# Expert rows fetched by token number, found by one-hot products, and the attention's work moved to other steps

## What is computed

```
xn = layernorm(x)
gnn: h = xn @ W;  out[col] += h[row] * dinv[row] * dinv[col]  over the edges and self loops
mix: q, k, v = xn @ w_qkv + b_qkv;  A = q k^T * SCALE
     numerator = 1 + A + 0.5 A*A;   attn = numerator / numerator.sum(-1)
     out = (attn v) @ w_proj + b_proj
x = x + gnn + mix
xf = layernorm(x)
probs = softmax(xf @ switch_w + switch_b);  prob_max, routes = max, argmax
rank = position of the token among those of its expert, by falling prob_max
keep = rank < 195
buf[route, rank] = xf                  (kept tokens only)
h = gelu(buf @ w1 + b1);  o = h @ w2 + b2
y = o[route, rank] where kept, else xf
x = x + y * prob_max
```

## Time and profile before

| | us |
|---|---|
| median of 3 runs | 1110.61 (1110.03 to 1113.11) |
| the profiled execution | 1114.51 |
| its span | 1112.6 |
| TensorE busy in the span | 933.1 (84%) |
| VectorE busy | 773.2 (69%) |
| ScalarE busy | 483.2 (43%) |
| GpSimd busy | 342.0 (31%) |

### The profile page before, as it was taken

The page is one execution under the profiler, slowest core; times in us unless marked ns, Lnnn a source line. Parts: engine busy times, 40 slices in busy tenths (PEclk is TensorE's granted clock), DMA queues, the critical chain, the costliest instruction groups (busy, mean ns, idle before and its releaser), DMA issues.

```text
span 1112.6 us, 15566 instructions
## 1 busy us (share of the span) xinstructions
PE 933.1 (84%) x5250; PEld 887.4 (80%) x5250; DVE 773.2 (69%) x1557; ACT 483.2 (43%) x710; POOL 342.0 (31%) x223
## 2 busy tenths in 40 slices
PE   3897789989989989989998779699999983197885
PEld 3896778878878978878987679699999982197885
DVE  6778168889878889878887635646676666067673
ACT  2221256656656656656667402112232222154540
POOL 2025555544546546534344000000000002323342
PEclk9898899999999999999999889899999995599898
DMA  8966443283273273285463374554545424786761
GB/s 235 350 181 144 85 88 49 36 153 56 28 153 49 35 153 52 32 173 118 120 133 70 47 164 108 135 134 110 146 114 144 109 70 152 214 268 213 232 223 45
DMA packets 139572, 142.44 MB, mean 128 GB/s; under 512 B 71418, under 2 KB 119133, under 8 KB 138503
## 3 DMA queue, kind: packets, MB, share of 16 engines
q1 hardware_dynamic: 110628, 125.01, 42.7%
q0 software_dynamic: 28496, 16.68, 10.3%
q10 hardware_dynamic: 403, 0.17, 0.1%
HBM read 99.09 MB, written 42.97 MB: 128 GB/s over the span
## 4 chain that ended last, share of the span: by engine, by line
PE 51%; DVE 16%; issue 12%; DMA 9%; ACT 8%; POOL 1%; SPq 1%; DVEq 0%; ACTq 0%; POOLq 0%
PE ps L1872 12%; PE ps L1874 11%; PE ps L1873 11%; PE ps L1166 6%; PE ps L1150 3%; PE ps L1151 3%; ACT Ph L812 3%; DMA out<-oE,ids 3%; DVE Pl L1024 3%; DMA vdram<-VS 3%; ACT Pf L834 2%; DVE Ph L1022 2%; PE ps L1520 1%; DMA Cs<-counts 1%; DVE oE L1806 1%
## 5 line engine op out<-in xcount | busy, mean ns | idle before, releaser
L372 POOL DMA_INDIRECT counts<-countc,idxu x157 | 273.5, 1742 | 299.8 <-DMA counts<-countc,idxu 204.7
L1024 DVE SCALAR_TENSOR_TENSOR Pl<-Pf,Ph 125x832 fp32r<-125x832 f32 (+1 forms) x180 | 184.4, 1026 | 65.0 <-ACT Ph L812 58.9
L834 ACT ACTIVATE Pf<-ps 125x832 f32<-125x832 f32 (+1 forms) x180 | 155.8, 866 | 147.1 <-PE ps L1151 140.1
L1166 PE MATMUL ps<-Ph,vsb 125*128 125x416 f32 (+1 forms) x360 | 132.1, 367 | 10.4 <-DVE Pl L1024 10.1
L1166 PE MATMUL ps<-Pl,vsb 125*128 125x416 f32 (+1 forms) x360 | 127.8, 355 | 0.0
L1663 POOL DMA_INDIRECT rows<-XF,slots x10 | 14.7, 1470 | 337.3 <-DVE slots L1479 334.6
L1872 PE MATMUL ps<-XH,wqkH 128*128 128x416 f32 (+1 forms) x216 | 81.3, 376 | 19.6 <-DVE R L942 9.9
L1872 PE MATMUL ps<-wH,XH 128*125 128x384 f32 x240 | 84.7, 353 | 10.5 <-DVE OHL L969 5.8
L1166 PEld LDWEIGHTS ps<-Ph,vsb 125*128 125x128 f32 x360 | 68.9, 191 | 20.7 <-DVE Pl L1024 10.6
L1873 PE MATMUL ps<-wL,XH 128*125 128x384 f32 x240 | 83.4, 348 | 0.0
L1874 PE MATMUL ps<-wH,XL 128*125 128x384 f32 x240 | 83.2, 346 | 0.0
(11 more groups left out here) (247 smaller groups left out, 2243.5 us busy)
## 6 DMA issues: line engine op xcount, KB each, us to landing
Cs<-counts SPq DMA_DIRECT2D x20, 546.9 KB
w1s<-L_ffn_w SPq DMA_DIRECT2D x8, 1152.0 KB
w2s<-L_ffn_w SPq DMA_DIRECT2D x8, 1152.0 KB, 5.7
odram<-OHL SPq DMA_DIRECT2D x12, 625.0 KB, 8.5
oS<-odram SPq DMA_DIRECT2D x10, 750.0 KB, 4.8
vdram<-VS SPq DMA_DIRECT2D x10, 672.0 KB
vsb<-vdram SPq DMA_DIRECT2D x12, 560.0 KB
kt<-keyd SPq DMA_DIRECT2D x5, 1280.0 KB, 6.0
```

What stands on the lines that cost most here:

```text
L372: pool.indirect_dma_start(out=counts, out_offset=bass.IndirectOffsetOnAxis(ap=idxu[:, c:c + 1], axis=0), in_=countc[:, c:c + 1], in_offset ...
L834: act.activation(Pf[:, i % RING, :, 0:w], ps[0:T, 2 * (i % 2):2 * (i % 2) + 2, 0:w], ACT.Square, bias=1.0).then_inc(sq_done, 1)
L1024: dve.scalar_tensor_tensor(out=p, in0=f, scalar=1.0, in1=h.bitcast(F32), op0=ALU.add, op1=ALU.subtract).then_inc(p_lo, 1)
L1166: ins = pe.matmul(ps[:, 4 + s % 2, 0:w], vsb[:, 2 * kp + t, a, :], part[:, m % RING, t, 0:w], start=(kp == 0 and t == 0 and part is Ph), s ...
```

## The change

1. **Routing.** The seven operations for `slots` and the ten scatters to `rows` go. For each of the ten tiles VectorE writes `seat`, 125 tokens by 195 places, one where the token's rank is that place; TensorE multiplies it with the one-hot experts times token number and times top probability (`lg[:, 1:3]`, 16 columns), accumulated over the ten tiles, once for each of the two row tiles, and a one-row product adds 2097152 to the token numbers, which `tok` carries negatively, so that an empty place has a number out of bounds. VectorE casts the result to `ids` for all eight experts and copies `pmc`.
2. **Rows.** SyncE stores each tile of `XF` to the DRAM array `xfd` during the node tiles (`store_rows`); GpSimd gathers an expert's rows from it by `ids` (`fetch_rows`): experts 0 and 1 at the start, expert e+2 at the start of turn e, where SyncE had loaded them before. `rows`, `blank`, `clear` and the `r_zero` waits go.
3. **Order at the node tiles' end.** `add_ranks` and `compare` of the tiles before come ahead of the last tile's `logits` and `choose`; in `choose` the probability comes before the expert.
4. **Experts.** VectorE no longer waits for `oe_store` before `w2L`, only at `oE`; the copies of ids are replaced by one small operation on `pcur`. `w1L` of expert 0 comes first, and the `pads` wait for `plain_store`.
5. **Attention.** The step tables change, and all three quadratic products use bank 6, so that the first projection step waits for the queries' reading (`kq_full`) instead of the second quadratic's (`r_done`).

The diff, cut to its core:

```
-        XF, = right(ctx, [("XF", [T, NT, RW], F32)])
+        XF, = right(ctx, [("XF", [T, NT, D], F32)])
...
-            sp.wait_ge(consts, 1)
-            sp.dma_start(blank.rearrange("(p d) -> p d", p=2), zeros[0:2, 0:RW]).then_inc(r_zero, 16)
-            sp.wait_ge(r_zero, 16)
-            sp.dma_start(blank.rearrange("(p d) -> p d", p=2)[:, D + 1:RW], iota_f[0:2, 10:11],
-                         allow_slow_non_contiguous=True).then_inc(r_zero, 16)
...
-        QUAD_AT, TOTAL_AT, INVERSE_AT = (3, 5, 8), (11, 12, 13), 16
-        PROJ_AT, TURN_AT, GRAM_AT = (7, 13, 20, 24, 29), (24, 27, 30), 32
+        QUAD_AT, TOTAL_AT, INVERSE_AT = (1, 5, 9), (13, 14, 15), 18
+        PROJ_AT, TURN_AT, GRAM_AT = (7, 13, 19, 25, 30), (24, 27, 30), 32
...
-        READ_AT = (11, 16, 23, 27, 32)
+        READ_AT = (11, 16, 22, 28, 33)
...
-        FIRST_AT = (24, 25, 26, 28)
-        LATE_AT = (2, 5)
+        FIRST_AT = (23, 25, 26, 29)
+        LATE_AT = (0, 5)
...
-                        if i == PROJ_AT[0]:
-                            pe.wait_ge(r_done, 3 * j + 2)
+                            pe.wait_ge(kq_full, 6 * j + 6)
...
+            def store_rows(i):
+                sp.wait_ge(xf_done, i + 1)
+                move(sp, xfd[i * T:(i + 1) * T, :], XF[:, i, :], xf_store)
...
+            add_ranks(NT - 3)
+            compare(NT - 2)
...
             logits(NT - 1)
             choose(NT - 1)
-            add_ranks(NT - 3)
-            compare(NT - 2)
             add_ranks(NT - 2)
             compare(NT - 1)
             add_ranks(NT - 1)
...
+            for i in range(NT):
+                dve.tensor_scalar(seat[:, i, :], place[:], rank[:, i:i + 1], None, ALU.is_equal).then_inc(seat_done, 1)
+            for t, (r0, n) in enumerate(CTILES):
+                dve.wait_ge(seat_mm, t + 1)
+                dve.tensor_copy(ids[0:n, t, :], ps[0:n, 2 * t, 0:E]).then_inc(ids_done, 1)
...
+            for t, (r0, n) in enumerate(CTILES):
+                for i in range(NT):
+                    pe.wait_ge(seat_done, i + 1)
+                    pe.matmul(ps[0:n, 2 * t, 0:2 * E].rearrange("p (a e) -> p a e", a=2), seat[:, i, r0:r0 + n], lg[:, 1:3, i, :],
+                              start=(i == 0), stop=False)
+                pe.matmul(ps[0:n, 2 * t, 0:2 * E], later[0:1, 1:1 + n], far[:].rearrange("p a e -> p (a e)"), start=False,
+                          stop=True).then_inc(seat_mm, 1)
...
-            for i in range(NT):
-                pool.indirect_dma_start(out=rows, out_offset=bass.IndirectOffsetOnAxis(ap=slots[:, i:i + 1], axis=0),
-                                        in_=XF[:, i, :], in_offset=None, bounds_check=SLOTS - 1, oob_is_err=False
-                                        ).then_inc(sent, 16)
...
+            def fetch_rows(e):
+                for t, (r0, n) in enumerate(CTILES):
+                    pool.indirect_dma_start(out=xe[0:n, e % 2, t, :], out_offset=None, in_=xfd,
+                                            in_offset=bass.IndirectOffsetOnAxis(ap=ids[0:n, t, e:e + 1], axis=0),
+                                            bounds_check=N - 1, oob_is_err=False).then_inc(xe_in[e % 2], 16)
...
             for e in range(E):
+                if e + 2 < E:
+                    pool.wait_ge(xe_tr, 3 * e + 3)
+                    fetch_rows(e + 2)
...
-                        dve.wait_ge(oe_store, e + FREE)
-                        ids_of(e + 1, 1 - b, m * 32 + 32 * (b + 1))
+                        dve.wait_ge(oe_done, 2 * e + FREE)
+                        chance_of(e + 1, 1 - b)
                         split_w2(e + 1, 1 - b)
```

146 lines of the change are left out of this document (67 added, 79 removed).

## The result

| | before | after |
|---|---|---|
| median, us | 1111.46 (1110.03 to 1113.11, 4 runs) | 1080.79 (1076.30 to 1081.14, 4 runs) |
| profiled execution, us (span) | 1114.51 (1112.6) | 1076.30 (1074.5) |
| mean granted clock of TensorE | 0.937 | 0.952 |

The ratio is 0.9714, with a 95% interval of 0.9685 to 0.9744: 31 us faster. That is inside the range given for 8 in 10 (1044 to 1083), outside the forecast's own (1051 to 1072), 19 us above the predicted time and 4 above rival A's. The profiled execution of after is 4.4 us faster than the other three, which lie within 0.5 us of each other. The mean granted clock of those three is 0.942 to 0.946, and six experiments have profiles of the same attention code; by these the 4.4 us are most likely the clock of the attention. (The change of clock meant here is between 1.0 and 0.5 of full speed, 2.4 and 1.2 GHz.)

The account below looks back on a forecast made before the run. TensorE was taken to bound node tiles and nearly the attention, a circle through the results' landing the expert turns. Gains of 22 + 1 + 15 + 11 = 49 us gave 1110.6 - 49 = 1061.6 us; own range 1051 to 1072, 8 in 10 1044 to 1083.

Parts of the forecast that it names:

- rival A: Attention: VectorE becomes the bound, only 7 us of wait MA stay, the rest returns as waits for Pl; 1076.6 us, 18%.
- attention, five turns: Attention turns with a projection: 4.1 us gained in each of five, from moving work off three TensorE waits.
- routing: Last router logits to first expert: place products and gathers replace scatters and load; 15 us gained, bounds 10 and 18.
- experts: Expert turns: w2L leaves the circle, turns of 15.3 instead of 17.47 us; 11 us gained, bounds 2 and 18.
- I take 4.1 of the 5.7 us: Attention: share of the 5.7 us a turn expected to stay, since VectorE, at 88% of the turn, is late next.
- The three waits: TensorE in the attention: for MA at step 5 (1.5 us), R at step 7 (2.0), kt at the gram product (1.2).
- The 1.0 us of clock a turn: Attention: granted clock falls to 0.50 behind the wait for R; removing that wait regains 1.0 us a turn.
- the last argument: Experts: the second store, issued later beside a weight load, lands in a little less than 6.4 us; 15.3 taken.
- Rival B: Experts: GpSimd's queue is the bound, w1L holds the first store every turn, nothing gained there; 1072.6 us, 12%.
- Rival C: Whole kernel: everything runs at TensorE's pace, 67 us gained; 1043.6 us, 13%.
- Rival D: Experts: the two new gathers delay each store by two landings of 6.1 us, circle 26.5 us; 1127 us, 1%.
- The signs of being wrong: Edge-count scatters ending behind the attention, node tiles over 192 us, or gathers landing only after 955.

Follow-up runs that it names:

- a_load: The changed kernel with three compares of edge keys done twice, at steps 7, 8 and 10 of a pair: 1099.28 us.
- b_again: The kernel before, unchanged, run once more for a second profiled execution: 1110.33 us.
- r_fill: The changed kernel with GpSimd's two fills of xe behind the ten seat operations instead of beside the last tile's choice: 1080.01 us.
- e_behind: The changed kernel with the two gathers of expert e+2's rows behind the stores and x1 gathers instead of ahead of the first store: 1135.43 us.
- e_ahead: The changed kernel with the two row gathers at the end of GpSimd's turn, for expert e+3 instead of e+2: 1078.59 us.
- e_w1late: The changed kernel with w1L of the next expert behind the three hL in VectorE's turn instead of ahead of them: 1081.39 us.
- r_free: The changed kernel with w1L of the first expert and the last two plain rows ahead of the casts of ids: 1079.13 us.
- e_wait: The changed kernel with w2L again behind the landing of the results of the expert before: 1094.34 us.
- a_later: The changed kernel with compares of edge keys moved from steps 7 to 10 to where VectorE has gaps: 1075.38 us.

## Why the prediction was right in its range and wrong in its size

| step | predicted gain | measured |
|---|---|---|
| first stage | 1 | 1.7, likely (108.6 to 106.9) |
| attention, five turns | 20.5 | 8.5 (422.1 to a median of 413.7) |
| attention, last turn | 1.5 | 1.2 (73.2 to 72.0) |
| node tiles | 0 | 0 within scatter |
| routing | 15 | 11.3 (55.2 to 43.9) |
| experts | 11 | 9.0 (17.47 to 15.67 a turn, five turns) |
| sum | 49 | 31.7; the medians say 31 |

**Attention, the step that failed: "I take 4.1 of the 5.7 us".** The three waits went as described, some 23 us in the five turns (the earlier trace rows without the waits for `MA` of the first pair and of the last turn). What failed is what was late next. The prediction named VectorE with 88% of the turn, and then let the 58.9 us for which VectorE idled for `Ph` speak for room; the 4.1 itself stands on no row. Only some of those microseconds lie in steps 3 to 13, where TensorE was to come forward. The largest of them stands at step 9. Timeline of DVE before, in the second turn and in the third, where the clock had fallen:

```profile
250.88 1.03 DVE L1024 SCALAR_TENSOR_TENSOR Pl<-Pf,Ph 125x832 fp32r<-125x832 f32 x1 [2.72 <-ACT Ph L812]
...
335.34 1.03 DVE L1024 SCALAR_TENSOR_TENSOR Pl<-Pf,Ph 125x832 fp32r<-125x832 f32 x1 [4.28 <-ACT Ph L812]
```

The waits for `MA` and `R` that were removed ahead of it are 3.5 us a turn, more than the gap of 2.7; with the clock, about 5 against 4.3. In after that gap is used up, VectorE has none from step 3 to 13, and a_load shows that a microsecond added there costs TensorE a whole one. So 14 of the 23 us came back as waits for `Pl`, `kt` and `inv` (idling fell from 39.0 only to 30.2): 1.7 us a turn were kept, not 4.1. That is rival A in its mechanism for steps 3 to 13, VectorE the bound with waits for `Pl`, and nearly in its size (7 us for the whole attention against 9.7). Behind step 13 the waits for `inv` and for `kt` ahead of the transposes grew by some 3 us each, which A doesn't explain; their cause stays open.

**The 1.0 us of clock a turn** The earlier trace rows was counted as regained because its wait, for `R`, goes. It was read in one turn and taken for all five. The clock fell in three of them, for some 3 us each, and in two in b_again; with about 1.5 us a fall, 1.0 a turn comes out for the first profile by luck. Windows of 5 us in the third turn, of r_fill and then of after:

```profile
335.00:340.00 5.00, 5.00 (x26) 4.87 (x26) 2.69 (x6) 1.76 (x2) 3.09 (x2) 0.77 0.44 79
```

```profile
335.00:340.00 5.00, 5.00 (x34) 4.95 (x33) 3.64 (x8) 2.64 (x3) 3.15 (x2) 1.00 0.42 79
```

In r_fill the clock falls behind the new wait of 1.3 us at step 13, in three turns of five; in e_behind, e_ahead, e_w1late and r_free also in three, in e_wait in two, in the profiled execution of after in none. TensorE's busy time in the five turns is 383.5 in r_fill, 384.1 before: this gain wasn't had. It is as large as the 4.4 us by which the profiled execution of after beats the other three, and a_later, whose wait at step 13 is at most 0.67, has it.

**Routing: 15 predicted, 11.3 measured, from errors of both signs.** The place products took less than 9.3 us: 6.97 for 40 of the 44 records, and `ids` were complete 8.4 us behind the ranks instead of 10.1, 1.7 better. The ranks came only 0.5 us earlier, not 1.9, and r_fill shows why: the fills of `xe`, costed at nothing without naming who runs beside them, held one small VectorE operation for 2.6. From `ids` to the transposes it is 13.6 us instead of 9.5, 4.1 worse: the hold of the first gather was foreseen, but the second one started 5.8 us behind `ids`, and its landing took 7.7 us instead of the median of 6.1; r_free, without the hold, has 10.7. Part of the 4.1 is a slip in the sum: it has the gathers issued by 948.4, so the second at 947.4, and the median landing makes that 953.5, not the 951.8 that it goes on with. By its own rows it was 13.3 us, not 15. Together 1.7 - 1.4 - 4.1 = -3.8. The bounds, 10 to 18, held; the sign given for `ids`, 7 us behind the ranks, wasn't the sum's 10.1, and 8.4 lies between.

**Experts: mechanism right, 9.0 us of the 11.** `w2L` left the circle (e_wait puts it back and pays 2.7 us a turn), the first store slipped into `w1L` in every turn but the first, TensorE's waits for `oE` are 1.2 to 1.8 us (under 2, as said), and 15.7 us lie between the 15.3 chosen and the 15.8 that the sum gave before the last argument, that the second store would land sooner. That argument wasn't borne out, and for the 0.15 in the sum the prediction gives no row. Rival B had the first store right, but not that this takes all. Rival C needed free stores: e_ahead has the first one free and comes to 14.3 us a turn. Rival D said that a gather delays a store behind it by its landing; in after the stores land 6.5 us (median) from their issue, with two gathers in front, so it doesn't. But e_behind shows the other side of the same choice: put last, the gathers are on TensorE's path, and the turn is 24.4 us.

The Trainium skill, "SBUF — State Buffer", section "Who interferes with whom", infers that writing descriptors needs the write interface of the pair that VectorE and GpSimd share; by that inference `w1L` would have held none of these transfers. The rows contradict it once more (4.23 us beside `w1L` in after, 1.00 in e_w1late where `w1L` runs elsewhere), and the sum was right to go by the row.

**The median and one profile.** The prediction subtracted from the median, which was right. The two profiled executions alone would say 38 us; 4.4 of these are most likely the clock of the attention in one of them, and 3.1 are that the other was that much slower than its median.

**The signs of being wrong.** None came: the last scatter of edge counts is issued at 585.7 us, 29 before the attention's end (600.49 and 31 before); the stretch with the node tiles takes no longer than before; the first gathers have landed by 937. The turns of the attention were to take 79 to 80 us and take 82.7.

## What to carry to other kernels

When waits of one engine are removed, look at the engine that is next by place, not by sum: draw its timeline over the very steps from which work is moved, and count the gaps there. Idle time elsewhere in the turn isn't room, and a gap at the very place is room only up to its own length. Where a transfer is placed in a queue, price it both ways: what it delays behind it, and when its own reader wants it. With the same two gathers the turn is 15.7 us where they stand ahead of the stores, 24.4 where they stand behind them, and 15.0 (14.2 to 14.5 from the third turn on) where they stand behind but are fetched a turn earlier. And small fills on an engine that idles aren't free if they hold an operation of a neighbour on the critical path.

## What the runs showed of the hardware

- A VectorE operation of 125x8 numbers, begun 0.09 us before the first of two fills on GpSimd by the profile, ended only with the second: 2.81 us instead of 0.23, 903.36 to 906.17, the fills until 906.15. With the fills moved it took 0.23. The Trainium skill, "SBUF — State Buffer", section "Who interferes with whom", counts such an operation among those that can take the ports it shares with GpSimd, and says that whichever issues first keeps them for its whole instruction while the other fully blocks. The trace agrees with the block; with the order only if the start of 903.36 isn't yet the taking of the ports, since the fill starts later, at 903.45. That the operation stayed blocked across two fills issued one after the other was not expected; r_free shows the same, 2.81 us again.
- In the other direction, an indirect transfer issued beside `w1L` (2.55 us) takes until 0.9 to 1.1 us after that operation's end: 976.21 to 980.44 with `w1L` until 979.30 in after, 990.38 to 992.35 with `w1L` until 991.43 in e_w1late. Moved out of it, it takes 1.0 us.
- Waits of TensorE of 1.25 to 1.45 us at step 13 stand ahead of a fall of the granted clock from 1.0 to 0.5 in some turns and executions and not in others, and so do those of 2.0 for `R` (three turns of five in before, two in b_again). In a_later, with waits of 0.56 to 0.67 there, no fall was seen in five turns; in a_load, with 2.8 to 3.0, one in each of five. What else decides isn't settled by these runs. The price of it: TensorE's busy time for the same products was 379.1 us with no fall, 382.1 with two, 383.5 to 383.6 with three and 385.2 with three of which one was long, in executions of the same attention code.
